# Gate and up as three float16 products in the feed-forwards of a macaron block

## The reference

```
def fp4_quant_dequant(x):            # blocks of 16 along the last dim
    scale = max(|block|) / 6, at least 1e-12
    q = nearest of 0, 0.5, 1, 1.5, 2, 3, 4, 6 to |x/scale|, times sign and scale
fp4_linear(x, w) = einsum(quant(x), quant(w))
ffn(x)  = fp4_linear(silu(fp4_linear(x, w_gate)) * fp4_linear(x, w_up), w_down)   # 256 -> 704 -> 256
x = x + 0.5 * ffn(layernorm(x))
x = x + attention(layernorm(x))      # 16 heads of 16, T = 2048
x = x + 0.5 * ffn(layernorm(x))
```

## Time and profile before

| | us |
|---|---|
| median of 3 runs | 3876.11 (3875.68 to 3876.95) |
| profiled execution | 3876.43 |
| its span, first to last instruction | 3874.6 |
| TensorE busy | 3739.6 (97%) |
| VectorE busy | 3483.9 (90%) |
| ScalarE busy | 2798.9 (72%) |
| GpSimd busy | 2185.0 (56%) |
| mean granted TensorE clock | 0.991 |

### The profile page before, as it was taken

How to read it: one execution, slowest core, us unless ns; L and a number is a source line. 1 busy time by engine, 2 the same in 40 slices (tenths; PEclk the granted TensorE clock), 3 DMA queues, 4 the chain that set the end, 5 groups by cost and what they waited for, 6 DMA issues and landing times. The chain is left out here.

```text
span 3874.6 us, 64196 instructions
## 1 busy us (share of the span) xinstructions
PE 3739.6 (97%) x21885; PEld 1463.3 (38%) x21885; DVE 3483.9 (90%) x6466; ACT 2798.9 (72%) x3614; POOL 2185.0 (56%) x3450
## 2 busy tenths in 40 slices
PE   5999999999999999999999999999999999999999
PEld 3777775422222222222222222222222222777776
DVE  8999984689999999999999999999999994898887
ACT  3444444379989989998998998998998998244443
POOL 2334430057677767776777776776777773243333
PEclk8999999999999999999999999999999999999999
DMA  4000002211010110011101001001001000100000
GB/s 156 1 1 4 1 1 82 83 41 30 21 42 21 30 32 30 21 30 32 30 21 39 24 28 35 26 25 34 28 24 37 24 29 13 38 17 17 17 17 23
DMA packets 71807, 116.50 MB, mean 30 GB/s; under 512 B 29304, under 2 KB 50744, under 8 KB 69560
## 3 DMA queue, kind: packets, MB, share of 16 engines
q1 hardware_dynamic: 71480, 112.40, 10.1%
HBM read 73.99 MB, written 28.58 MB: 26 GB/s over the span
## 5 line engine op out<-in xcount | busy, mean ns | idle before, releaser
L1382 DVE TENSOR_REDUCE stats<-ps_b 128x1 f32<-128x512 f32 x3577 | 2263.3, 683 | 66.2 <-PE ps_b L1435 24.1
L1373 ACT ACTIVATE probs<-ps_s 128x1024 f32<-128x1024 f32 x2048 | 1995.6, 1025 | 224.9 <-PE ps_s L1448 211.3
L1435 PE MATMUL ps_b<-w_ffn 48*128 48x512 f16 x4016 | 1237.6, 384 | 72.0 <-DVE stats L1382 45.4
L1448 PE MATMUL ps_s<-w_ffn 51*128 51x512 f16 x4096 | 1168.7, 382 | 3.5 <-PEq L1011 1.7
L1461 PE MATMUL ps_o<-probs,w_qkvT 128*32 128x512 f32 x8192 | 1099.1, 609 | 0.1
L1435 PEld LDWEIGHTS ps_b<-w_ffn 48*128 48x128 f16 x4016 | 308.2, 93 | 1287.1 <-DVE stats L1382 1231.9
L1310 POOL TENSOR_TENSOR w_ffn<-w_ffn 128x256 f32<-128x256 f32 x878 | 519.8, 592 | 265.3 <-ACT w_ffn L1358 230.8
L1312 POOL TENSOR_SCALAR w_ffn<-w_ffn 128x256 f32<-128x256 f32 x878 | 600.1, 683 | 76.9
L884 PE MATMUL ps_gu_f<-w_ffn,zT_f 128*128 128x352 f32 x2048 | 629.7, 460 | 1.3 <-DVE x_res L1585 0.9
L1314 POOL TENSOR_TENSOR w_ffn<-w_ffn 128x256 f32<-128x256 f32 x878 | 517.6, 589 | 73.4
L884 PEld LDWEIGHTS ps_gu_f<-w_ffn,zT_f 128*128 128x128 f32 x2048 | 380.2, 191 | 192.3 <-issue 2.7
(11 more groups left out here) (169 smaller groups left out, 3077.6 us busy)
## 6 DMA issues: line engine op xcount, KB each, us to landing
w_ffn<-qk_parts_dram SPq DMA_DIRECT2D x256, 128.0 KB
w_ffn<-qk_parts_dram SPq DMA_DIRECT2D x256, 64.0 KB
qk_parts_dram<-factor SPq DMA_DIRECT2D x32, 256.0 KB, 2.5
qk_parts_dram<-first_group SPq DMA_DIRECT2D x32, 256.0 KB, 2.5
factor<-denom_dram SPq DMA_DIRECT2D x64, 128.0 KB, 5.2
out<-x_res SPq DMA_DIRECT2D x16, 512.0 KB, 2.7
v_then_heads<-y SPq DMA_DIRECT2D x224, 32.0 KB
x_res<-in_L_attn_x SPq DMA_DIRECT2D x3, 2048.0 KB, 18.6
```

Of the source, the lines that this page charges most:

```text
L1373: nc.scalar.activation(probs[:, (2 * at + j % 2) % PROBS, :], ps_s[:, j % 2, :], ACT.Exp, scale=head_scale[g % H]).then_inc(exped, 1)
L1382: nc.vector.tensor_reduce(mx[:, head % SLOTS, k // 4, k % 4:k % 4 + 1], ps_b[:, n % RING, :], AX.X, ALU.max).then_inc(bank_reduced, 1)
L1435: last = nc.tensor.matmul(ps_b[j:j + STRIP, n % RING, :], Q[s][M, qt * P + j:qt * P + j + STRIP], K[s][M, kb * 512:(kb + 1) * 512], start= ...
L1448: last = nc.tensor.matmul(ps_s[j:j + STRIP, half, (c % 2) * 512:(c % 2 + 1) * 512], K[slot][0:ROWS, kt * P + j:kt * P + j + STRIP], Q[slot ...
```

## The change

The quantised weights of gate and up are scaled by a power of two and kept as a float16 part and a float16 rest; so is z. Gate and up become three products of float16: high by high, low weights by high z, high weights by low z. The scale is taken back in silu's factor, in a floor for h's scale and in down's weights. h and its rounding are left as they were.

In the weights stage a largest weight is found over all partitions (a transpose, a reduction, a product with a row of ones), powers of two are made of it, and VectorE makes the low parts from PSUM. The excerpts (a line "..." marks what is left out):

```diff
+                pe.wait_ge(largest_ready, 1)
+                nc.tensor.transpose(ps[0:1, 7, 0:P], gmax[:], m.ident[:]).then_inc(largest_turned, 1)
+                pe.wait_ge(ones_set, 1)
+                pe.wait_ge(largest_alone, 1)
+                nc.tensor.matmul(ps[:, 6, 0:1], ones[:], power[0:1, :], start=True, stop=True).then_inc(largest_spread, 1)
...
+                    dve.wait_ge(largest_turned, 1)
+                    nc.vector.tensor_reduce(power[0:1, :], ps[0:1, 7, 0:P], AX.X, ALU.max).then_inc(largest_alone, 1)
...
+                    dve.wait_ge(largest_spread, 1)
+                    link(nc.vector.tensor_scalar(gmax[:], ps[:, 6, 0:1], SMALLEST, None, ALU.max))
+                    link(nc.vector.tensor_scalar(gmax[:].bitcast(I32), gmax[:].bitcast(I32), EXPONENT, None, ALU.bitwise_and))
+                    link(nc.vector.reciprocal(power[:], gmax[:]))
+                    link(nc.vector.tensor_scalar(power[:], power[:], W_GROWTH * (1.0 + 2.0**-12), None, ALU.mult))
+                    link(nc.vector.tensor_scalar(power[:].bitcast(I32), power[:].bitcast(I32), EXPONENT, None, ALU.bitwise_and))
+                    nc.vector.tensor_scalar(m.tiny[:], power[:], TINY * Z_GROWTH, None, ALU.mult).then_inc(dve_step, 1)
+                    nc.vector.tensor_scalar(m.w_back[:], gmax[:], 1.0 / (W_GROWTH * Z_GROWTH), None, ALU.mult).then_inc(dve_step, 1)
+                    nc.vector.tensor_scalar(m.silu_scale[:], gmax[:], -1.0 / (SHRINK * W_GROWTH * Z_GROWTH), None, ALU.mult).then_inc(dve_step, 1)
+                    n[0] += 3
+                    link(nc.vector.tensor_scalar(scale[:, at], scale[:, at], power[:, 0:1], None, ALU.mult))
...
+                nc.vector.tensor_reduce(gmax[:], amax[:], AX.X, ALU.max).then_inc(largest_ready, 1)
...
+                for j, to in lows:
+                    dve.wait_ge(kept, j + 1)
+                    nc.vector.tensor_tensor(to, ps[:, j % 8, 0:to.shape[-1]], jobs[j][1], ALU.subtract).then_inc(lows_kept, 1)
...
+        self.link(dve, nc.vector.tensor_scalar(self.scale, self.scale, self.m.w_back[:, 0:1], None, ALU.mult), 3)
```

In the feed-forward, ScalarE (the scale of silu is now a register, loaded at the stage's start):

```diff
+                silu_scale = nc.scalar.alloc_register(f"silu_scale_{tag}")
+                nc.scalar.reg_load(silu_scale, m.silu_scale[0:1, 0:1].bitcast(I32))
...
+                    if live(2):
+                        act.wait_ge(pool_z, (i + 3) * PZ_STEPS)
+                        if live(0):
+                            act.wait_ge(zT_turned, i + 1)
+                        nc.scalar.copy(z_parts[:, q, 0:D], zq[:, q, :]).then_inc(z_high, 1)
                     for a in range(2 if live(0) else 0):
...
-                        nc.scalar.activation(half(silu, a), gate[:, a], ACT.Silu, scale=-1.0 / SHRINK).then_inc(silu_done, 1)
+                        nc.scalar.activation(half(silu, a), gate[:, a], ACT.Silu, scale=silu_scale).then_inc(silu_done, 1)
```

VectorE (the second rounding of z and the update of x move ahead of the rounding of h; the same instructions):

```diff
                         nc.vector.scalar_tensor_tensor(out=zr[:], in0=zA[:], scalar=ROUNDER, in1=zs[:, q, :],
                                                        op0=ALU.max, op1=ALU.add).then_inc(z_round, 1)
+                    if live(2):
+                        dve.wait_ge(z_round, (i + 2) * R_STEPS + 1)
+                        nc.vector.scalar_tensor_tensor(out=zr[:], in0=zA[:], scalar=ROUNDER, in1=zr[:],
+                                                       op0=ALU.max, op1=ALU.subtract).then_inc(z_round, 1)
+                    if old:
+                        t = i - UPDATE
+                        dve.wait_ge(dn_done, t + 1)
+                        nc.vector.scalar_tensor_tensor(out=m.x[:, t, :], in0=ps_dn[:, t % 2, 0:D], scalar=0.5 / SHRINK**2,
+                                                       in1=m.x[:, t, :], op0=ALU.mult, op1=ALU.add).then_inc(x_done, 1)
                     if live(-1):
                         dve.wait_ge(h_abs, i)
...
-                    if live(2):
...
-                    if old:
...
-                        nc.vector.tensor_scalar(hscale[:, q, :], hamax[:], SHRINK / 6.0, TINY, ALU.mult, ALU.max).then_inc(h_step, 1)
+                        nc.vector.tensor_scalar(hscale[:, q, :], hamax[:], SHRINK / 6.0, m.tiny[:, 0:1], ALU.mult, ALU.max).then_inc(h_step, 1)
```

GpSimd (at the end of its step) and TensorE:

```diff
+                    if live(3):
+                        pool.wait_ge(z_high, i + 4)
+                        nc.gpsimd.tensor_tensor(z_parts[:, 1 - q, D:], zq[:, 1 - q, :], z_parts[:, 1 - q, 0:D], ALU.subtract).then_inc(z_low, 1)
...
-                    pe.wait_ge(pool_z, (i + 2) * PZ_STEPS)
+                    pe.wait_ge(z_low, i + 2)
...
-                    for k in range(KD):
-                        last = nc.tensor.transpose(ps_zT[:, k * P:(k + 1) * P], zq[:, 1 - q, k * P:(k + 1) * P], m.ident[:])
+                    for k in range(2 * KD):
+                        last = nc.tensor.transpose(ps_zT[:, k * P:(k + 1) * P], z_parts[:, 1 - q, k * P:(k + 1) * P], m.ident_half[:])
...
                             for k in range(KD):
-                                for c in (a, 2 + a):
-                                    last = nc.tensor.matmul(ps_gu[:, c, 0:HW], zT[:, q, k * P:(k + 1) * P],
-                                                            m.w_guT[:, k, c * HW:(c + 1) * HW], start=(k == 0), stop=(k == KD - 1))
+                                for part, w in ((0, m.w_gu_high), (0, m.w_gu_low), (1, m.w_gu_high)):
+                                    for c in (a, 2 + a):
+                                        last = nc.tensor.matmul(ps_gu[:, c, 0:HW], zT[:, q, (part * KD + k) * P:(part * KD + k + 1) * P],
+                                                                w[:, k, c * HW:(c + 1) * HW], start=(k == 0 and w is m.w_gu_high and part == 0),
+                                                                stop=(k == KD - 1 and part == 1))
```

More of the change, by code:

```diff
@@ L87 @@
 SMALLEST = 2.0**-50
+W_GROWTH = 2.0**14
+Z_GROWTH = 2.0**10
 GROUP = P // DH
@@ L175, in weights_phase @@
         gu_quantised = sem("gate_up_quantised")
-        turned, kept = sem("w_turned"), sem("w_kept")
+        ones_set, largest_ready, largest_turned, largest_alone, largest_spread = (
+            sem(n) for n in ("ones_set", "w_largest_ready", "w_largest_turned", "w_largest_alone", "w_largest_spread"))
+        ones, gmax, power = sb("ones_row", [1, P]), sb("w_largest", [P, 1]), sb("w_power", [P, 1])
+        lows = []
+        turned, kept, lows_kept = sem("w_turned"), sem("w_kept"), sem("w_lows_kept")
         jobs = []
@@ L212, in _ @@
             def _(pool):
+                nc.gpsimd.memset(ones[:], 1.0).then_inc(ones_set, 1)
                 nc.gpsimd.memset(m.ident[:], 0.0).then_inc(ident_zero, 1)
@@ L441, with __init__ @@
     VAR_STEPS, ALL_STEPS = 7, 12
-    def __init__(self, nc, m, ctx, tag, home):
-        self.nc, self.m = nc, m
+    def __init__(self, nc, m, ctx, tag, home, growth):
+        self.nc, self.m, self.growth = nc, m, growth
         self.mean, self.diff, self.var, self.root, self.corr = (home[:, k * NT:(k + 1) * NT] for k in range(5))
@@ L627, in ffn_phase @@
         zscale, zinv = (small[:, (1 + 2 * k) * XB:(3 + 2 * k) * XB].rearrange("p (a b) -> p a b", a=2) for k in range(2))
-        zT = sb("zT", [P, 2, KD * P])
+        zT = sb("zT", [P, 2, 2 * KD * P], F16)
+        z_parts = sb("z_parts", [P, 2, 2 * D], F16)
         warm = sb("silu_warm", [P, 1])
@@ L640, in ffn_phase @@
         ps_T = bank("ps_T", [P, 1024])
[L641 removed]
+        ps_hT, ps_zT = ps_T[:, 0:(PAIR - EVEN) * P], ps_T[:, (PAIR - EVEN) * P:].bitcast(F16)
         ps_dn = bank("ps_dn", [P, 2, 512])
@@ L654, in ffn_phase @@
         R_STEPS = 2
-        H_STEPS = 8
+        H_STEPS = 7
         gate = ps_gu[:, 0:2, 0:HW]
@@ L768, in step @@
                         nc.vector.tensor_tensor(half(h, a), up[:, a], half(silu, a), ALU.mult).then_inc(h_step, 1)
-                    if old:
-                        t = i - UPDATE
-                        dve.wait_ge(dn_done, t + 1)
-                        nc.vector.scalar_tensor_tensor(out=m.x[:, t, :], in0=ps_dn[:, t % 2, 0:D], scalar=0.5 / SHRINK**2,
-                                                       in1=m.x[:, t, :], op0=ALU.mult, op1=ALU.add).then_inc(x_done, 1)
                     if here:
@@ L1606, in program @@
         m.w_ffn = sb("w_ffn", [P, KD * 2 * I + PAIR * D])
-        m.w_guT = m.w_ffn[:, 0:KD * 2 * I].rearrange("p (k i) -> p k i", k=KD)
+        m.w_gu_high, m.w_gu_low = (m.w_ffn[:, part * KD * I:(part + 1) * KD * I].bitcast(F16).rearrange("p (k i) -> p k i", k=KD)
+                                   for part in range(2))
+        m.tiny, m.w_back, m.silu_scale = (sb(n, [P, 1]) for n in ("h_tiny", "w_back", "silu_scale"))
         m.w_dnT = m.w_ffn[:, KD * 2 * I:].rearrange("p (c d) -> p c d", d=D)
@@ L1642, in program @@
         m.y_ready = y_and_norm.enter_context(nc.semaphore("y_ready"))
-        norm = Norm(nc, m, y_and_norm, "n2", m.va[:, 6 * S:])
+        norm = Norm(nc, m, y_and_norm, "n2", m.va[:, 6 * S:], 1.0)
```

36 lines of the change are left out of this document (17 added, 19 removed).

## The result

The changed kernel takes 3978.14 us (median of 3 runs, 3974.55 to 3978.93) against 3876.11: a ratio of 1.0264, 95% interval 1.025 to 1.0278. It is 102 us slower. The forecast was 3880, its range 3845 to 3915.

The account below looks back on a forecast made before the run. TensorE bounds the kernel now and VectorE would next, at 7.66 us a plain tile of the second feed-forward. From 3878.0, including +14.2 and -12.6 for the feed-forwards, plus 2 for thin cover and column floor: 3880 us, range 3845 to 3915.

Parts of the forecast that it names:

- VectorE, a tile: VectorE's time per feed-forward tile: links +0.34, GpSimd collisions -0.12 and +0.36, so 7.06 becomes 7.66 us in second feed-forward.
- The sum over VectorE: VectorE's plain tile: 7.66 us in the second feed-forward, 7.85 in the first, more in steps with extra statistics.
- the floor from a tile of one column: L784 on VectorE takes its floor from a one-column tile: bounds 0 and 0.1 us, taken as 0.
- The two signs: The feed-forwards move in opposite directions: first +14.2 us, second -12.6.
- the sum of +1.6: Both feed-forwards together, +14.2 and -12.6: 1.6 us slower.
- TensorE's start and tile: First gate and up starts near 54 us, before at 47.42; TensorE's feed-forward tile falls from 8.13 to 6.9 us.
- The tile of 6.9: TensorE's feed-forward tile falls from 8.13 to 6.9 us, its 24 float16 products taking 3.5 instead of 4.74.
- The loop of z: z's added float16 copy and subtraction stay hidden: about 4.0 us against VectorE's 4.15 in second feed-forward's plain tiles.
- z's low part comes late: Rival: GpSimd's subtraction takes 0.8 us or more, L750 is late, a plain tile becomes 8.1, total 3912 us; 20%.
- silu hidden by 0.7: On ScalarE, z's float16 copy and silu end after 1.6 us; VectorE asks for silu after 2.3, so hidden by 0.7.
- The clock: A granted clock under 1.00 in the feed-forwards, where TensorE now pauses, would be a cost not counted; no size given.

Follow-up runs that it names:

- two kernels that lose it in different ways: The changed kernel with the update of x back behind h's products (3895.76 us), and with it left in place but a step later (3896.17 us).
- The 3896: The changed kernel with the update of x one step later, all else in the order of the change: 3896.17 us, ratio 1.0054.
- the fastest kernel: Changed kernel, update a step later, VectorE scaling z after both its roundings, ScalarE's Abs of z first, GpSimd's product taking z to scale last: 3848.29 us.
- the new order: Changed kernel, update a step later; VectorE: z's first rounding, update, second rounding, z's scale, h's roundings; ScalarE's Abs of z first: 4010.51 us, ratio 1.0355.

## Why the prediction was wrong

The failed step stands under "VectorE, a tile": "No instruction is added in the loop, but the order changes, and with it two things." There were three. The moved update brought its wait for down's product along, to a place where both roundings of h and all that follows on GpSimd and TensorE are queued behind it. I priced the update's neighbours (links, 0.11 each) and its length, not its wait. Before, it stood behind h's products, where VectorE idled for silu anyway. The wait costs 82 of the 102 us, shown by two kernels that lose it in different ways; in float32, without any low part, the same wait costs some 33 (3928 to 3895). The fall of the clock that comes with it is part of the 82. It could have been seen beforehand: with `UPDATE` 4 and `DOWN` 3 the even tile's `dn_done` is signalled in the same step, by TensorE, after gate and up of that step.

*The sum over VectorE* holds where the wait is gone. Plain tile of the second feed-forward: forecast 7.66, measured 7.76. The records are those forecast: L799 0.72 (0.72), L808 1.19 (about 1.25). The 0.1 is L829, the floor from a tile of one column, which I put at 0, and which also runs beside GpSimd's subtraction:

```profile
3704.29 0.89 DVE L835 TENSOR_TENSOR h_scaled_f<-h_f,h_inv_f 128x704 f32<-128x704 f32 x1
...
3706.32 0.72 DVE L799 SCALAR_TENSOR_TENSOR z_rounded_f<-z_abs_f,z_rounded_f 128x256 f32<-128x256 f32 x1
...
3707.30 1.19 DVE L808 SCALAR_TENSOR_TENSOR h_scaled_f<-factor,h_scaled_f 128x704 f32<-128x704 f32 x1
...
3711.24 0.31 DVE L829 TENSOR_SCALAR h_scale_f<-v_then_heads,h_tiny 128x44 f32<-128x44 f32 x1
...
3712.05 0.89 DVE L835 TENSOR_TENSOR h_scaled_f<-h_f,h_inv_f 128x704 f32<-128x704 f32 x1
```

(Timeline of VectorE, update a step later.) It is 0.25 with nobody beside it and 0.31 beside L868; the form with a constant, L784 before, takes 0.19. The prediction took L784 (now L829) for a neighbour that wouldn't slow the subtraction, which holds (0.67), and didn't ask what the subtraction does to it.

*The two signs* hold as well without the wait: first feed-forward +21.1 at its end (forecast +14.2), second from first to last tile -5.4 (forecast -12.6 with 1.65 for its start, so -14.2 without it). The starts were forecast at 7.6 and are 9.5; between the two 4.2 instead of 1.65. So without the wait the sum of +1.6 would have been missed by 20 us (the span is 21.5 longer). The 3896 would have lain in the range of 3845 to 3915, but only because the range is wide. This part of the miss is of sizes: some 2 us at the start, 5 in the first feed-forward, 2.5 between the two and 9 in the second.

*TensorE's start and tile*: the first gate and up was expected near 54. In the changed kernel, the first half of the 24 products:

```profile
54.13 3.70 PE L933 MATMUL ps_gu_f<-w_ffn,zT_f 128*128 128x352 f16 x12 [0.68 <-ACT zT_f L720]
```

It starts where expected, at a granted clock of 0.50 (53 to 58 us), so 12 products take what 24 take later. The 24 take 3.58 at full clock, forecast 3.5. The tile of 6.9 was too short: in the fastest kernel two tiles of TensorE without a wait take 14.13 (3706.22 to 3720.35), 7.07 each. The shortest tile measured on average is 7.22, where VectorE and TensorE both bound it.

*The loop of z*: hidden, as forecast, once the wait is gone. With the wait z's low part is on the path, but as a link of the update's ring. The rival "z's low part comes late" named the right victim for another reason; its subtraction was to take over 0.8 us and takes 0.67. *silu hidden by 0.7*: right in the changed order, and undone by either order in which z's rounding or its product comes later.

*The clock*: the prediction named a fall as an uncounted cost. It came with the waits and mostly went with them: 21 slow groups in the changed kernel, 3 with the update a step later.

By the Trainium skill (SBUF — State Buffer, "Who interferes with whom") the instruction that issues first keeps the shared port, and "Issue order, not op shape, decides who blocks." The runs agree in both directions: VectorE's L808 at 1.19 beside a GpSimd product that began earlier, and GpSimd's L855 at 1.14 behind a VectorE rounding that began 0.16 earlier. The prediction used the rule in both directions (L815 behind L764, 1.19); the expectation for the new order priced it on VectorE alone, and was wrong by 110 us and more.

## What to carry to other kernels

When an instruction is moved in an in-order queue, its wait moves too: find when its signal comes, in the step and by which engine, and what stands behind it in the new place; a wait that was free behind an idle spot can close a ring. If the signal comes in the same step, take the work a step later. When two engines share a path to memory, place the shorter queue's instructions beside those that don't read two operands from SBUF, price a collision for both sides, with all that is queued behind the loser, and measure the small neighbours too: here two tensor_scalars with one tensor operand paid as well (L802, L829). And a faster engine pays only after the next one has been made short enough: here the same float16 products range from 115 us lost to 28 gained.

## What the runs showed of the hardware that I had not expected

- A small tensor_scalar of 128x44 with its second operand from a tile of one column took 0.25 us alone, with a constant 0.19.
- A tensor_scalar of 128x16, 0.17 alone, took 0.37 beside a GpSimd product that had begun 0.29 earlier (L802 above); the 128x44 form with a column operand took 0.65 on average beside such a product and 0.23 without (L829, 110 to 260 us of the first feed-forward). The reductions and the products that read PSUM showed no such loss (L821 at 0.89, L818 two in 0.95, beside the 1.39 of GpSimd's product).
- In the changed kernel, where TensorE paused for up to 2.6 us ahead of a tile (56.9 us in 39 tiles), the granted clock of the feed-forwards' stretches was 0.92 to 0.98, and single groups of 24 products took 5.4 instead of about 3.7 us (clock 0.72 from 3714 to 3720), so some of it ran at 1.2 and not 2.4 GHz. With the update a step later (29.8 us in 43 tiles) the stretch from 3500 to 3840 had 1.00 and none of this.
